# Stage changes without a meeting of engines, and the norm there in two halves of the tokens

## The chip, the cores and the metric

The kernel runs on one core of one Trainium2 chip. The metric is the device time of one execution in microseconds (us). The kernel before took 1945.89 us, the median of three runs (1944.5 to 1947.28).

## What is computed

Four layers of a small transformer, each with cross attention, self attention and a feed-forward part: twelve sublayers over 32 x 32 = 1024 tokens of width 256, all in fp32. Between sublayers the pattern is always the same:

```python
x = x + sublayer(_layernorm(x, axis=-1), ...)
```

The sublayers differ: softmax attention, an attention with query sets, capped attention, a "resonance" attention, and routed experts. Two details matter here. The first feed-forward part (`l0_feed_forward`) normalises the normed rows once more, by their root mean square, with a scale vector; it picks one of 8 experts by distance to centroids of those rows, and adds the result to the layer-normed rows and x. Some sublayers norm a second time with a mean and variance of their own, which for rows that are normed already is the same as another epsilon and factor in the first root.

## The kernel before, in words

The 1024 tokens stand as 8 tiles of 128 rows (`core.X`, [128, 8, 256]). Each sublayer is a *stage*: a Python function (`l0_cross`, `l0_self`, `l0_feed_forward`, then `l1_...`, `l2_...`, `l3_...`) that opens one block, in which each of the five engines has its own instruction stream. Semaphores order them. In this text the stages are called by their tile prefixes: l0x, l0a, l0f, l1x, l1a, l1f, l2x, l2a, l2f, l3x, l3a, l3f (x cross attention, a self attention, f feed-forward). There is no planner: the order on each engine is the order in which the code is written.

**The tail of a stage.** TensorE (PE) multiplies the last output projection, two tiles at a time. VectorE (DVE) adds each pair to X, and `Norm.take` (L227, L230) computes `bn_stats` and `bn_aggr` for these tiles, so that means and variances are ready when the stage ends. ScalarE (ACT) loads the table for the square root (`load_table`, L242). PE runs filler matmuls on constants (`keep_busy`, L83).

**The change of stage.** The end of a block is a meeting of all engines; `free_sems` (L89) then lets GpSimd (POOL) clear the stage's semaphores and makes all engines meet a second time.

**The head of a stage.** PE runs filler again. ACT takes the root of the variances of all eight tiles (`Norm.scalar`, L259), DVE the reciprocal (`Norm.deviations`, L237) and the shift (L195), and then both write the normed rows H: DVE five tiles (L197), ACT three (L206). PE transposes the rows tile by tile (`Flip.tensor`, L292) into four PSUM banks, ACT copies two of these to HT (L305, L309) and DVE the other two (L320, L324), and `Flip.ready` holds PE's first projection until all four copies are done. SyncE (SP) starts the loads of the next stage's weights behind the meeting.

**l0f.** Behind the H rows, ACT squares and sums them (L2089) and takes a root (L2091), DVE makes the rows R (L2111), PE transposes R, ACT squares R for its lengths (L2095), PE computes the distances (`route_tile`, L1253), and DVE and PE sort the tokens by expert (`Places`). DVE then adds H to X (L2131), POOL gathers the sorted rows with indirect DMAs (`move_rows`, L1023), and PE transposes them (L1054) ahead of the experts' matmuls.

**l2f.** Four pairs of experts in a hardware loop on PE and DVE; its tail does not call `take`, so the head of l3x computes the statistics of all eight tiles (L181, L217).

**l3x and l3a.** l3x multiplies a bias vector by the value weights (16 small matmuls, L3474) in front of the transposes. l3a norms twice: rows H for the values, then rows in `at.Q` for queries and keys, with a second transposition; its projections (L384 for queries and keys, L389 for values) run tile by tile in turn.

Of the kernel before, what the change touches and what calls it, by code (L numbers as in the profile page):

```python
# [26 lines left out]
ROWS_BY_DVE, ROWS_BY_ACT = (0, 2, 4, 6, 7), (1, 3, 5)  # L27
EXPERTS = {2: (8, 3072, 0), 5: (9, 5136, D), 11: (6, 2052, D)}
SHARED = 5
FIRST_PARTS = (0, 4 * D, 4 * D + 2 * D + 8 + P + 2 * B + 1 + C * B, 4 * D + 2 * D + 8 + P + 2 * B + 1 + C * B + 5 * D)  # L30


class Core:


    def __init__(self, nc, es, dram):
        self.nc, self.es, self.dram = nc, es, dram
        self.sems = []
# [4 lines left out]
        self.weights = [self.sb("weights0", [P, 6424]), self.sb("weights1", [P, 10640])]  # L43
# [6 lines left out]
        self.eps = self.sb("eps", [P, 3])  # L50
# [13 lines left out]
        self.eps5, self.eps10, self.eps6 = (self.eps[:, i:i + 1] for i in range(3))  # L64
        self.x_in = self.sem("x_in")
        self.shared_in = self.sem("shared_in")
        self.vectors_in, self.rest_in = self.sem("vectors_in"), self.sem("rest_in")
        self.norm = Norm(self)
        self.flip = Flip(self)
        self.ctx_norm = ContextNorm(self)  # L70
        self.sems = []
# [4 lines left out]
    def sem(self, name):  # L76
        self.sems.append(self.nc.alloc_semaphore(name=name))
        return self.sems[-1]
# [81 lines left out]
class Norm:  # L160
# [3 lines left out]
    def __init__(self, core):  # L164
        self.core = core
# [3 lines left out]
        self.uses_dve = self.uses_act = self.shifts_dve = self.shifts_act = 0  # L169
        self.taken = False  # L170

    def vector(self, dve, src, dst, rows_done):

        c, nc = self.core, self.core.nc
        if src is c.X and self.taken:
            dve.sem_inc(self.moments_done, 1)  # L176
            self.deviations(dve)
            self.taken = False
        else:
            for t in range(NT):  # L180
                done = nc.vector.bn_stats(c.stats[:, t, :], src[:, t, :])  # L181
            c.dve_step(dve, done)
            self.statistics(dve)
        self.rows(dve, src, dst, rows_done)

    def rows(self, dve, src, dst, rows_done):
        c, nc = self.core, self.core.nc
        if not isinstance(rows_done, tuple):
            for t in range(NT):
                nc.vector.tensor_scalar(dst[:, t, :], src[:, t, :], c.moments[:, t, 0:1], c.rstd[:, t:t + 1],  # L190
                                        ALU.subtract, ALU.mult).then_inc(rows_done, 1)
            return
        dve_done, _ = rows_done
        self.shifts_dve += 1
        nc.vector.scalar_tensor_tensor(c.shift[:], c.moments[:, :, 0], -1.0, c.rstd[:], ALU.mult, ALU.mult).then_inc(self.shift_done, 1)  # L195
        for t in ROWS_BY_DVE:
            nc.vector.tensor_scalar(dst[:, t, :], src[:, t, :], c.moments[:, t, 0:1], c.rstd[:, t:t + 1],  # L197
                                    ALU.subtract, ALU.mult).then_inc(dve_done, 1)

    def scalar_rows(self, act, src, dst, rows_done):  # L200
        c, nc = self.core, self.core.nc
        _, act_done = rows_done
        self.shifts_act += 1
        act.wait_ge(self.shift_done, self.shifts_act)
        for t in ROWS_BY_ACT:
            nc.scalar.activation(dst[:, t, :], src[:, t, :], ACT.Identity, bias=c.shift[:, t:t + 1], scale=c.rstd[:, t:t + 1]).then_inc(act_done, 1)  # L206

    def wait_rows(self, eng, rows_done):
        dve_done, act_done = rows_done
        eng.wait_ge(dve_done, len(ROWS_BY_DVE))  # L210
        eng.wait_ge(act_done, len(ROWS_BY_ACT))

    def statistics(self, dve):

        c, nc = self.core, self.core.nc
        for t in range(NT):
            done = nc.vector.bn_aggr(c.moments[:, t, :], c.stats[:, t, :])  # L217
        done.then_inc(self.moments_done, 1)
        self.deviations(dve)

    def take(self, dve, written, tiles):
# [7 lines left out]
        for t in tiles:  # L229
            nc.vector.bn_aggr(c.moments[:, t, :], c.stats[:, t, :])  # L230
        self.taken = True

    def deviations(self, dve):
        c, nc = self.core, self.core.nc
        self.uses_dve += 1
        dve.wait_ge(self.std_done, self.uses_dve)
        c.dve_step(dve, nc.vector.reciprocal(c.rstd[:], c.std[:]))  # L237
# [6 lines left out]
    def scalar_twice(self, act):  # L244


        self.scalar(act, self.core.eps10, 1 + 1e-5)

    def vector_again(self, dve, src, dst, rows_done):

        dve.sem_inc(self.moments_done, 1)
        self.deviations(dve)
        self.rows(dve, src, dst, rows_done)

    def scalar(self, act, eps, scale=1.0):
        c, nc = self.core, self.core.nc
        self.uses_act += 1
# [4 lines left out]
class Flip:  # L262
# [10 lines left out]
    def tensor(self, pe, src, rows_done, order=None):  # L273
# [3 lines left out]
        if self.uses["pe"]:  # L277
            self.ready(pe, "pe")
# [2238 lines left out]
def l1_self(core, load_next):  # L2517
# [20 lines left out]
    with ExitStack() as es:  # L2538
# [41 lines left out]
        def _(pe):  # L2580
# [79 lines left out]
            for m in range(FIRST):  # L2660
                project(m)
# [1428 lines left out]
```

## Time and profile before

| | |
|---|---|
| median of three runs | 1945.89 us |
| profiled execution, span from its first to its last instruction | 1943.1 us |
| TensorE, busy share of the span | 93% |
| DVE | 55% |
| ACT | 42% |
| POOL | 28% |
| mean granted TensorE clock | 0.971 |

The profile gives no time of its own for the profiled execution beyond the span; the span is 2.8 us below the median of the runs. The busy share of TensorE holds the filler matmuls and the time in which a matmul waits in its pipeline, so it isn't a share of useful work. A granted clock of 1.00 is 2.4 GHz and 0.50 is 1.2 GHz.

### The profile page before, as it was taken

The numbers are of one execution on the slowest core, as the hardware profiler recorded it, in microseconds if no ns is written. First come the engines' busy times: TensorE is split into PE (matmuls) and PEld (weight loads), VectorE is DVE, ScalarE is ACT, GpSimd is POOL, SyncE is SP. The second block draws the span as 40 slices with busy tenths as digits, with TensorE's granted clock in tenths as the row PEclk, the third lists the DMA queues.
The fourth block names the chain that finished last, engine by engine and source line by source line (L and its number), as shares of the span: only waits on it lengthen the run. The fifth ranks groups of instructions, "written<-read, shape, count | busy, mean of one in ns | idle before, by whom it ended". The sixth has DMA issues, their size and how long they took to land. (4 is left out here: it accounts for less than half of the span.)

```text
span 1943.1 us, 43256 instructions
## 1 busy us (share of the span) xinstructions
PE 1799.9 (93%) x16836; PEld 1400.7 (72%) x16836; DVE 1059.5 (55%) x2671; ACT 825.1 (42%) x2373; POOL 547.0 (28%) x586
## 2 busy tenths in 40 slices
PE   8999879999999989799999999999688899997898
PEld 6886568944777756699999967777454477755787
DVE  7786761163366437966555545555754555437511
ACT  6664521132166424333333335554510566626332
POOL 4440113200144302311222113332202456515242
PEclk9999778999999999999999999999799999998999
DMA  4110057662134110042899732111011345300397
GB/s 148 56 57 5 2 198 275 241 186 92 43 102 105 43 55 3 3 154 86 298 335 332 279 121 97 46 50 61 2 55 59 98 153 157 104 1 2 123 338 252
DMA packets 87010, 233.92 MB, mean 120 GB/s; under 512 B 9776, under 2 KB 45136, under 8 KB 80304
## 3 DMA queue, kind: packets, MB, share of 16 engines
q1 hardware_dynamic: 78992, 213.90, 32.5%
q0 software_dynamic: 5664, 15.47, 2.4%
q8 instruction: 121, 1.98, 0.4%
q10 hardware_dynamic: 2176, 2.10, 0.3%
q14 instruction: 57, 0.47, 0.1%
HBM read 216.21 MB, written 12.07 MB: 117 GB/s over the span
## 5 line engine op out<-in xcount | busy, mean ns | idle before, releaser
L2222 POOL TENSOR_TENSOR l1x_probs<-l1x_probs,l1x_total 128x512 f32<-128x512 f32 x64 | 65.1, 1038 | 203.7 <-DVE l1x_total L2461 203.7
L1541 PE MATMUL PS<-weights,l0x_ctxT 128*128 128x256 f32 x512 | 121.3, 387 | 0.0
L1074 PE MATMUL PS<-l1f_xT,l1f_slot 128*128 128x128 f32 x1024 | 117.0, 275 | 0.0
L1074 PEld LDWEIGHTS PS<-l1f_xT,l1f_slot 128*128 128x128 f32 x1024 | 115.7, 192 | 0.1
L83 PE MATMUL PS<-consts 128*128 128x256 f32 x366 | 90.8, 401 | 15.9 <-PEq L89 14.2
L1541 PEld LDWEIGHTS PS<-weights,l0x_ctxT 128*128 128x128 f32 x512 | 94.4, 191 | 15.2 <-issue 2.7
L2992 POOL TENSOR_TENSOR l2x_probs<-l2x_probs,l2x_total 128x512 f32<-128x512 f32 x64 | 65.0, 1038 | 127.1 <-DVE l2x_total L3182 127.1
L83 PEld LDWEIGHTS PS<-consts 128*128 128x128 f32 x366 | 72.3, 202 | 31.0 <-issue 18.3
L259 ACT ACTIVATE std<-moments,eps 128x8 f32<-128x8 f32 x13 | 3.9, 301 | 191.7 <-DVEq L176 122.3
L1201 DVE SCALAR_TENSOR_TENSOR l1f_product<-PS,l1f_slot,l1f_side 128x128 f32<-128x128 f32 x128 | 36.0, 344 | 65.9 <-ACT l1f_side L1157 65.9
L3496 PE MATMUL PS<-l3x_keysT,l3x_QW 128*128 128x289 f32 x256 | 67.7, 407 | 1.7 <-issue 1.7
L1028 POOL DMA_INDIRECT l1f_out_dram<-l1f_out,l1f_sort_target_row x23 | 22.7, 985 | 159.5 <-DVE l1f_out L1184 159.5
L1157 ACT ACTIVATE l1f_side<-PS,l1f_slot 128x128 f32<-128x128 f32 x128 | 36.5, 368 | 66.0 <-PE PS L1074 66.0
L1721 ACT ACTIVATE l0x_sq<-PS 128x256 f32<-128x256 f32 x128 | 47.8, 385 | 32.7 <-PE PS L1541 32.6
L3520 PE MATMUL PS<-tagged,l3x_QT 128*128 128x256 f32 x256 | 60.6, 380 | 0.9 <-ACT tagged L3610 0.9
L1074 PE MATMUL PS<-HT,weights 128*128 128x128 f32 x512 | 60.6, 280 | 0.9 <-DVE l1f_gated L1206 0.7
L3020 PE MATMUL PS<-l2x_ctxT,weights 128*128 128x257 f32 x256 | 61.1, 381 | 0.0
L1074 PEld LDWEIGHTS PS<-HT,weights 128*128 128x128 f32 x512 | 59.8, 196 | 1.7 <-DVE l1f_gated L1206 1.1
L1201 DVE SCALAR_TENSOR_TENSOR l1f_product<-PS,weights,l1f_side 128x128 f32<-128x128 f32 x120 | 33.8, 344 | 49.0 <-ACT l1f_side L1157 48.9
L3028 PE MATMUL PS<-weights,l2x_ctxT 128*128 128x256 f32 x256 | 60.4, 379 | 0.0
L3127 ACT ACTIVATE l2x_probs<-PS,l2x_top 128x257 f32<-128x257 f32 x128 | 59.2, 482 | 1.3 <-DVE l2x_top L3176 1.3
L1157 ACT ACTIVATE l1f_side<-PS,weights 128x128 f32<-128x128 f32 x120 | 34.2, 367 | 59.2 <-PE PS L1074 59.2
(663 smaller groups left out, 4630.9 us busy)
## 6 DMA issues: line engine op xcount, KB each, us to landing
l1f_slot<-in_experts_up_dram SPq DMA_DIRECT2D x16, 2056.0 KB, 10.5
weights<-in_experts_up_dram SPq DMA_DIRECT2D x8, 2056.0 KB, 10.4
weights<-in_experts_down_dram SPq DMA_DIRECT2D x21, 640.0 KB, 5.8
weights<-in_experts_up_dram SPq DMA_DIRECT2D x10, 1024.0 KB, 8.2
l1f_slot<-in_experts_down_dram SPq DMA_DIRECT2D x16, 640.0 KB, 4.8
l0x_ctxT<-in_ctxT_dram SPq DMA_DIRECT2D x32, 257.0 KB, 2.6
l1x_ctxT<-in_ctxT_dram SPq DMA_DIRECT2D x32, 257.0 KB, 2.9
l2x_ctxT<-in_ctxT_dram SPq DMA_DIRECT2D x32, 257.0 KB, 2.6
```

The costliest lines, as they stand in the source:

```text
L83: self.nc.tensor.matmul(self.PS[:, bank, 0:2 * P], self.ident, self.consts[:, 0:2 * P], start=True, stop=True)
L1074: done = nc.tensor.matmul(PS[:, bank + a, m * P:(m + 1) * P], mat[:, c, m * P:(m + 1) * P], x, start=(c == 0), stop=(c == 1))
L1157: nc.scalar.activation(self.side[u][:, m, :], PS[:, 2 * u, m * P:(m + 1) * P], ACT.Identity, bias=w["b1"][:, 4 * u + m:4 * u + m + 1]).the ...
L1201: done = nc.vector.scalar_tensor_tensor(p[:, m, :], PS[:, 2 * u + 1, m * P:(m + 1) * P], w["b3"][:, 4 * u + m:4 * u + m + 1], self.side[u] ...
L1541: last = nc.tensor.matmul(PS[:, 2 * (b % 2) + k, half * D:(half + 1) * D], ctxT[b % SLOTS][:, c, half * P:(half + 1) * P], kw[:, c, k * D: ...
L2222: nc.gpsimd.tensor_tensor(p, p, bcast(total[b % 2][:, 2 * n:2 * n + 2], 2, KEYS), ALU.mult).then_inc(probs_done, 1)
L2992: nc.gpsimd.tensor_tensor(p, p, bcast(total[b % 2][:, 2 * n:2 * n + 2], 2, 2 * P), ALU.mult).then_inc(probs_done, 1)
L3020: last = nc.tensor.matmul(PS[:, 4 + 2 * o, 0:CTX], wk[:, c, o * P:(o + 1) * P], ctxT[b % 2][:, c, :], start=(c == 0), stop=(c == 1))
L3028: last = nc.tensor.matmul(PS[:, 5, half * D:(half + 1) * D], ctxT[b % 2][:, c, half * P:(half + 1) * P], wv[:, c, :], start=(c == 0), stop ...
L3127: done = nc.scalar.activation(probs[b % 2][:, u, :], PS[:, u, 0:CTX], ACT.Exp, bias=top[b % 2][:, u:u + 1], scale=-1.0, accum_out=total[b ...
L3496: done = nc.tensor.matmul(PS[:, 2 * (b % 2) + u, 0:KEYS], QW[:, c, b, 4 * u:4 * u + 4, :].rearrange("p h q -> p (h q)"), keysT[b % 2][:, c ...
L3520: nc.tensor.matmul(PS[:, 6 + c, 0:2 * P], tokens[b % 2][:, half, c * P:(c + 1) * P], probsT[b % 2][:, half, :], start=(half == 0), stop=False)
```

## The change

It has five parts.

1. **No meeting.** All stages share one block. `leave` ends a stage: SP, ACT and DVE each drain and add one to a semaphore `left`, and POOL waits for the other four, clears the stage's semaphores, and adds one. PE adds its one behind the transposes of the first half (in `Flip.tensor`). `enter` waits for `left` before an engine first touches a semaphore of the new stage. Two ranges of semaphore numbers alternate. The last stage is not left.
2. **The norm by halves.** `Norm.take` signals after tiles 3 and 7. In the old stage's tail, DVE runs `early_vector` (reciprocal and shift for tiles 0 to 3) behind the third of its four additions, and ACT runs `early_scalar` (root, then the rows of tiles 0 to 3, all by ACT). In the new stage `scalar` and `vector` do tiles 4 to 7 (ACT tile 5; DVE tiles 4, 6, 7). PE transposes the first half at once; the projections of the first half come before the transposes of the second. Loops over (output, half) become loops over (half, output). In the three expert stages both halves are transposed before the router.
3. **Fillers.** `keep_busy` goes at the heads and tails of the stages, except 4 of 10 matmuls at the end of l0x; those inside the expert stages stay.
4. **l0f.** The second norm becomes part of the first root (another epsilon), the flip's copies multiply by the scale, POOL makes the rows R in two halves, and the addition of the layer-normed rows to X becomes eight `tensor_scalar` on POOL, in front of its gathers.
5. **Others.** l2f's last pair of experts is taken out of DVE's loop, with `take` in it. l3x's bias matmuls go behind the first context's work. l3a projects the values of tiles 0 to 3 ahead, and DVE alone writes the eight rows of the second norm. The start of the program is in the same block as l0x.

```diff
-ROWS_BY_DVE, ROWS_BY_ACT = (0, 2, 4, 6, 7), (1, 3, 5)
+ROWS_BY_DVE, ROWS_BY_ACT = (4, 6, 7), ((0, 1, 2, 3), (5,))
...
-    def free_sems(self):
-        self.nc.clear_and_free_semaphores(self.sems)
+    def enter(self, eng):
+        if self.stages:
+            eng.wait_ge(self.left, 5 * self.stages)
+
+    def leave(self):
+        nc, left, sems, others = self.nc, self.left, self.sems, 5 * self.stages + 4
+        @self.block.sync
+        def _(sp):
+            sp.drain().then_inc(left, 1)
...
+        @self.block.gpsimd
+        def _(pool):
+            pool.wait_ge(left, others)
+            nc.clear_and_free_semaphores(sems)
+            pool.drain().then_inc(left, 1)
         self.sems = []
-        self.nc.all_engine_barrier()
...
+    def early_scalar(self, act):
+        self.roots(act, self.use + 1, 0)
+        self.rows_by_scalar(act, self.use + 1, 0)
+
+    def early_vector(self, dve):
+        self.shifts(dve, self.use + 1, 0)
...
+    def project_tensor(self, pe, xT, wqk, wv):
+        flip = self.core.flip
+        flip.ready(pe, 0)
+        self.core.enter(pe)
+        self.project(pe, xT, xT, wqk, wv, (0, 1))
+        flip.tensor(pe, 1)
+        self.project(pe, xT, xT, wqk, wv, (2, 3))
+        flip.ready(pe, 1)
+        self.project(pe, xT, xT, wqk, wv, range(HALF, NT))
         self.turn_tensor(pe, 0)
         self.turn_tensor(pe, 1)
...
@@ l0_feed_forward, gpsimd
+            for half in range(2):
+                tiles = slice(HALF * half, HALF * half + HALF)
+                norm.wait_rows(pool, half)
+                nc.gpsimd.tensor_tensor(R[:, tiles, :], core.H[:, tiles, :], bcast(scale, 1, HALF), ALU.mult).then_inc(scaled, 1)
             ex.places.name_rows(pool)
+            pool.wait_ge(skips_done, 1)
+            for t in range(NT):
+                done = nc.gpsimd.tensor_scalar(core.X[:, t, :], core.X[:, t, :], more[:, t:t + 1], less[:, t:t + 1], ALU.mult, ALU.add)
+            done.then_inc(skipped, 1)
             ex.move_rows(pool)
...
@@ l1_cross, l3_cross and alike, tensor
-            pe.wait_ge(core.consts_in, 16)
-            core.keep_busy(7, 2)
+            flip.tensor(pe, 0)
+            core.enter(pe)
...
             for n in range(2 * HB):
-                o, half = n // 2, n % 2
+                half, o = divmod(n, HB)
+                if n == 2:
+                    flip.tensor(pe, 1)
+                if n == HB:
+                    flip.ready(pe, 1)
...
-            core.keep_busy(0, 4)
...
@@ l2_feed_forward, vector
+            add_pair(E // 2 - 1, 0)
+            dve.wait_ge(summed, (E // 2 + 1) * NT - HALF)
+            norm.take(dve, None, range(HALF))
+            add_pair(E // 2 - 1, 1)
+            norm.early_vector(dve)
+            dve.wait_ge(summed, (E // 2 + 1) * NT)
+            norm.take(dve, None, range(HALF, NT))
```

## Rows read from the trace of the kernel before

**Rows 1.** The page: span, busy time, and the group of the filler matmuls.
```profile
span 1943.1 us, 43256 instructions
PE 1799.9 (93%) x16836; PEld 1400.7 (72%) x16836; DVE 1059.5 (55%) x2671; ACT 825.1 (42%) x2373; POOL 547.0 (28%) x586
...
L83 PE MATMUL PS<-consts 128*128 128x256 f32 x366 | 90.8, 401 | 15.9 <-PEq L89 14.2
```

**Rows 2.** Windows, output to projection: us; PE, PEld, DVE, ACT, POOL busy; PEclk; DMA; GB/s.
```profile
177.00:189.00 12.00, 9.17 (x41) 7.16 (x39) 8.34 (x24) 4.29 (x12) 0.65 (x3) 0.86 0.04 14
253.00:265.00 12.00, 9.24 (x43) 6.85 (x42) 8.81 (x27) 5.13 (x21) 3.20 (x7) 0.95 0.77 308
382.00:401.00 19.00, 16.01 (x83) 13.59 (x81) 10.68 (x31) 3.44 (x6) 2.42 (x4) 1.00 0.40 124
693.40:700.60 7.20, 5.16 (x29) 3.64 (x28) 4.41 (x12) 2.99 (x6) 0.47 (x2) 1.00 0.45 148
826.60:832.70 6.10, 4.98 (x30) 3.68 (x28) 4.30 (x15) 2.85 (x6) 3.40 (x10) 1.00 0.41 121
1140.00:1148.20 8.20, 5.79 (x33) 4.03 (x32) 5.31 (x17) 3.42 (x7) 3.13 (x3) 1.00 0.22 68
1350.10:1357.40 7.30, 5.34 (x31) 4.02 (x29) 5.21 (x16) 2.99 (x6) 0.63 (x3) 1.00 0.50 160
1419.40:1427.00 7.60, 5.88 (x27) 4.64 (x26) 4.37 (x13) 3.08 (x7) 0.00 (x0) 0.82 0.54 203
1486.60:1500.30 13.70, 8.30 (x45) 7.19 (x45) 9.12 (x30) 3.49 (x7) 4.87 (x3) 0.88 0.56 176
1730.10:1741.70 11.60, 7.89 (x47) 5.78 (x46) 7.95 (x22) 6.34 (x12) 2.74 (x4) 1.00 0.01 2
1802.80:1810.00 7.20, 5.58 (x31) 4.03 (x29) 4.58 (x15) 2.86 (x6) 3.68 (x11) 1.00 0.10 36
```

**Rows 3.** Timeline, l1x to l1a: start, us, engine, line, operation.
```profile
694.40 0.18 DVE L230 BATCH_NORM_AGGREGATE moments<-stats 128x2 f32<-128x6 f32 x1
...
696.18 0.30 ACT L259 ACTIVATE std<-moments,eps 128x8 f32<-128x8 f32 x1 [21.62 <-DVEq L176]
...
696.95 1.59 ACT L206 ACTIVATE tagged<-X,shift,rstd 128x256 f32<-128x256 f32 x3 [0.47 <-DVE shift L195]
...
697.39 2.35 PE L292 MATMUL PS<-consts,tagged 128*128 128x128 f32 x16 [0.17 <-DVE tagged L197]
...
700.62 5.82 PE L2608 MATMUL PS<-HT,weights 128*128 128x512 f32 x13 [0.88 <-DVE HT L320]
```

**Rows 4.** Timeline, l2x to l2a: the third pair's moments.
```profile
1350.05 0.25 DVE L230 BATCH_NORM_AGGREGATE moments<-stats 128x2 f32<-128x6 f32 x2
```

**Rows 5.** Timeline, l0a to l0f: router, first gather, first transposition.
```profile
265.68 6.97 PE L1253 MATMUL PS<-l0f_centm,l0f_XT 128*128 128x8 f32 x32
...
286.48 3.14 POOL L1023 DMA_INDIRECT l0f_rows_in<-l0f_rows_dram,l0f_sort_token_row  x1 [27.43 <-DVE l0f_sort_token_row L858]
...
295.25 0.69 PE L1054 MATMUL PS<-consts,l0f_rows_in 128*128 128x128 f32 x2 [6.52 <-DMA l0f_rows_in<-l0f_rows_dram,l0f_sort_token_row]
```

**Rows 6.** L1023's gathers in l0f: from issue to landing.
```profile
DMA to landing us min/median/max: 2.8/6.8/8.7
```

**Rows 7.** Groups on POOL by form: busy, mean ns, idle before.
```profile
L1501 POOL TENSOR_SCALAR tagged<-X,moments,rstd 128x256 f32<-128x256 f32 x8 | 10.2, 1283 | 0.0
...
L3712 POOL TENSOR_TENSOR tagged<-tagged,weights 128x2048 f32<-128x2048 f32 x1 | 4.2, 4161 | 0.1
```

**Rows 8.** Timelines, l0f to l1x and l2f to l3x.
```profile
396.15 1.26 POOL L2216 TENSOR_SCALAR l1x_scaled_kv<-weights 128x128 f32<-128x128 f32 x2
...
1490.69 2.71 DVE L181 BATCH_NORM_STATS2 stats<-X 128x6 f32<-128x256 f32 x8 [2.22 <-PEq L89]
1491.63 1.84 PE L3474 MATMUL PS<-weights 128*128 128x1 f32 x16
```

**Rows 9.** Window inside l0a, columns as in rows 2.
```profile
216.00:233.00 17.00, 12.76 (x428) 9.51 (x428) 11.61 (x23) 13.58 (x29) 4.19 (x4) 0.50 0.01 3
```

More of the change, by code:

```diff
@@ L168, in __init__ @@
         self.shift_done = core.sem("norm_shift_done")
[L169 to L219, printed above, removed]
+        self.rows_act = core.sem("norm_rows_act")
+        self.rows_dve = core.sem("norm_rows_dve")
     def take(self, dve, written, tiles):
@@ L229, in take @@
         for t in tiles:
[L230 to L237, printed above, removed]
+            done = nc.vector.bn_aggr(c.moments[:, t, :], c.stats[:, t, :])
+        if tiles[-1] % HALF == HALF - 1:
+            done.then_inc(self.moments_done, 1)
     def load_table(self, act):
@@ new lines, in shifts, with rows_by_scalar @@
+    def shifts(self, dve, use, half):
+        c, nc = self.core, self.core.nc
+        tiles = slice(HALF * half, HALF * half + HALF)
+        dve.wait_ge(self.std_done, 2 * use + half + 1)
+        c.dve_step(dve, nc.vector.reciprocal(c.rstd[:, tiles], c.std[:, tiles]))
+        nc.vector.scalar_tensor_tensor(c.shift[:, tiles], c.moments[:, tiles, 0], -1.0, c.rstd[:, tiles], ALU.mult, ALU.mult).then_inc(self.shift_done, 1)
+    def rows_by_scalar(self, act, use, half):
+        c = self.core
+        act.wait_ge(self.shift_done, 2 * use + half + 1)
+        for t in ROWS_BY_ACT[half]:
+            c.nc.scalar.activation(c.H[:, t, :], c.X[:, t, :], ACT.Identity, bias=c.shift[:, t:t + 1], scale=c.rstd[:, t:t + 1]).then_inc(self.rows_act, 1)
@@ L327, in ready @@
-    def ready(self, eng, key, half=1):
-        eng.wait_ge(self.copied_act, 2 * self.uses[key] - 1 + half)
-        eng.wait_ge(self.copied_dve, 2 * self.uses[key] - 1 + half)
+        src, wait_row = c.H if src is None else src, wait_row or c.norm.wait_row
+        if nth:
+            self.ready(pe, half, nth - 1)
+        for ch in range(C):
+            for t in range(HALF * half, HALF * half + HALF):
+                if ch == 0:
+                    wait_row(pe, t)
+                last = nc.tensor.transpose(c.PS[:, 2 * half + ch, (t % HALF) * P:(t % HALF + 1) * P], src[:, t, ch * P:(ch + 1) * P], c.ident[:])
+            last.then_inc(self.flipped, 1)
@@ new lines, in tensor, with scalar @@
+        if half == 0 and nth == 0:
+            pe.drain().then_inc(c.left, 1)
+    def scalar(self, act, half, dst, scale=None, bias=None, nth=0):
+        c, nc = self.core, self.core.nc
+        act.wait_ge(self.flipped, 4 * (self.use + nth) + 2 * half + 1)
+        bank, to = c.PS[:, 2 * half, :], dst[:, 0, half * 512:(half + 1) * 512]
+        if scale is None:
+            last = nc.scalar.copy(to, bank)
+        elif bias is None:
+            last = nc.scalar.activation(to, bank, ACT.Copy, scale=scale[:, 0:1])
+        else:
+            last = nc.scalar.activation(to, bank, ACT.Identity, bias=bias[:, 0:1], scale=scale[:, 0:1])
+        last.then_inc(self.copied_act, 1)
@@ L2512, in _ @@
                 add_out(tiles)
+                if tiles == (4, 5):
+                    norm.early_vector(dve)
         cn.loads = B // cn.SLOTS
@@ L3526, in _ @@
             pe.wait_ge(q_copied, 2 * M)
+            for m in range(M):
+                for c in range(C):
+                    done = nc.tensor.matmul(PS[:, 7, m:m + 1], wv[:, c, m * P:(m + 1) * P], bm[:, c:c + 1], start=(c == 0), stop=(c == 1))
+            done.then_inc(v_bias_done, 1)
             for n in range(HEADS * C):
```

673 lines of the change are left out of this document (372 added, 301 removed).

## The prediction, as put on record before the result

> **What bounds the kernel now.** I read the page first. TensorE is busy for 93% of the span, no other engine for more than 55%, but 90.8 us of TensorE's time is filler on constants [rows 1]. So the question is where TensorE does nothing useful, and the change of stage is such a place, eleven times. The second view is the windows, each cut from a stage's last output matmul to the next stage's first projection [rows 2]. They hold 19.0 us at most (l0f to l1x, where most is the gather of the experts' rows), 6.1 at least (l1a to l1f) and 111.9 together. The only useful work of TensorE in one is 16 transposes (32 in l3a). The third view is the timeline of one change, l1x to l1a [rows 3]: the last moments are done at 694.58, the root starts at 696.18, because all engines meet twice in between, the transposes run from 697.39 to 699.74, and the first projection starts at 700.62, behind the last copy. The waits are in series, and TensorE is behind every one of them.
>
> **What limits TensorE behind the change.** From the last moments to the projection it is 6.0 us, and nothing of this can be hidden while the norm needs all eight tiles. With halves, the chain of tiles 0 to 3 can start when their moments are done, several us earlier. What then remains between the last output matmul and the first projection is: eight transposes (half of 1.9 to 2.4, so 1.0), one copy of 0.69 with its latencies, and beside the copy the leaving: DVE's and PE's drains, POOL's clearing, and the release of PE. The two meetings together take 1.6 us from the end of the moments to the start of the root [rows 3], and one of them goes, so I give the leaving 0.7 (bounds 0.5 and 1.6). The eight transposes of the second half now cost TensorE 1.0 behind the first projections, and that comes off each gain below, except where both halves stand ahead of the router.
>
> **Where TensorE ends late (l1a, l2f, l0a).** In l1a the rows of the first half are done before the last output matmul. The first projection is then at 693.4 + 1.0 + 1.1 = 695.5 in place of 700.6, less 1.0: a gain of 4.1. In l2f DVE's early reciprocal and shift fall in an idle stretch; the rows end at about 1420.8, the transposes at 1421.3, DVE's last moments at 1421.3, the projection starts at 1422.4 in place of 1427.0: 4.6 less 1.0, so 3.6. In l0a ACT's rows end near 182.1 and the projection starts at 183.8 in place of 189.1: 4.3.
>
> **Where DVE's last pairs run back to back (l2x, l2a, l1x).** Here the rows of the first half can only start behind the third pair, and the last pair is put back by 0.45 (reciprocal and shift). For l2a: third moments at 1350.3 [rows 4], shift done 1350.7, four rows by ACT at 0.53 each (three took 1.59 [rows 3]) to 1352.8, transposes to 1353.3, release 0.7, projection at 1354.1 in place of 1357.4: 3.3, and 2.5 are left, because DVE has one more copy between its rotations. l2x by the same steps: 1145.0 in place of 1148.2, less 1.0: 2.3 with rounding. l1x is the poor one. PE leaves only behind the transposes, at about 396.7, POOL clears then, and only then prepares the key weights, 1.46 us of memset and two multiplications (the latter 1.26 [rows 8]), which a matmul in front of the projections needs. That puts the projections at 399.5 in place of 401.0, less 1.0: 0.5. SP's loads of context also wait for POOL, about 1.4 us longer than before; I cost this at nothing because TensorE has 16 projections of some 0.86 us and the hidden layer in front of that context; if this cover is gone it is 1.4.
>
> **Where both halves come first (l1f, l3f).** Only the meetings and half of the rows are saved. The second half goes on from the end of DVE's last moments: root 0.35, reciprocal and shift 0.45, three rows 1.1, transposes 0.4, copies. The router can start on tiles 0 to 3 after the first copy: 1.8 in l1f, 2.2 in l3f.
>
> **l3x.** l2f's statistics (2.71 for eight tiles [rows 8], and the aggregates) leave the head. Rows by ACT from 1488.9 to 1491.1, transposes to 1491.5, first projection at 1492.5 in place of 1500.3: 7.8. Less 1.0 for the second transposes and less 1.84 for the bias matmuls, which lay in the shadow and are now on TensorE's path [rows 8]: 5.0. **l3a.** TensorE first does four value projections (1.03 each), but DVE alone makes eight rows at 0.34, and the queries and keys start at 1739.3 in place of 1741.6. DVE limits this phase, so the value work taken off TensorE isn't counted: 2.5.
>
> **l0f.** The squares, the second root and DVE's eight rows (3.26) leave the chain. POOL makes R instead: half of 4.16 each [rows 7], so 255.6 to 260.1, and ACT's squares of R end at 261.9. The router runs from 258.8 and takes 3.7 at full clock (as in l3f's head) or 7.0 at half as before, so it ends between 262.5 and 265.8; before, it ended at 272.65 [rows 5]: 6.9 to 10.2 gained. Part of this is given back: the eight `tensor_scalar` on POOL stand in front of its gathers. The nearest row is a POOL operation of this shape with two column operands, 1.28 us [rows 7], so 10.3 us, where DVE's one addition was 2.3 us and beside the path. The first gather was issued at 286.48 and its rows came at 295.2, 8.8 later, while the experts' weights were loading and DVE wrote [rows 5]. Now the issue stands 0.5 (three small DVE operations) and 10.3 us further behind the sorting, but the weights will have landed, and a gather lands 2.8 us from issue at the least [rows 6]: 0.5 + 10.3 + 2.8 - 8.8 = 4.8 lost. Net 3.5 (bounds 1 and 6). The Trainium skill, page GPSIMD Engine Reference, section 4.1 Engine selection, puts elementwise work on VectorE and calls GpSimd about two times slower for two inputs; by its measured 4.5 to 2.3 us for 2048 elements the eight would take 4.5 us, the gathers would hardly be late, and l0f would gain 8 to 9. The row of this shape says 10.3, and I go by the row.
>
> **Start and end.** One meeting at the start, and one meeting with a clearing at the end go: 1.0 (bounds 0.5 and 1.6).
>
> **The sum.** 4.3 (l0a) + 3.5 (l0f) + 0.5 (l1x) + 4.1 (l1a) + 1.8 (l1f) + 2.3 (l2x) + 2.5 (l2a) + 3.6 (l2f) + 5.0 (l3x) + 2.5 (l3a) + 2.2 (l3f) + 1.0 = 33.3 us.
>
> **The clock.** The fillers go, and with them activity of TensorE around each change. Even with them, the clock stood at half in four of eleven windows: 0.86 over 12.0 us is 3.4 us at 1.2 GHz [rows 2], and 16 transposes then took 3.7 in place of 2.35. So one such fall costs 1.4 to 1.7. The gaps that remain are shorter (2.5 us or less of idle), but nothing fills them. I count four more falls: 6 us. None is the lower bound, and in all eleven, with l0f longer, about 15 the upper. The Trainium skill, page TensorE: Matmul & The Clock Gate, section Why this matters for your kernels, says to keep TensorE free of gaps between bursts because an idle gap halves the clock; by that rule a fall follows each of the seven clean changes, 12 us in place of 6.
>
> Net 33.3 - 6 = 27.3. The profiled span would be 1943.1 - 27.3 = 1915.8. The median of the runs is 2.8 above the span, so 1918.6.
>
> **The rivals.**
> *The clock stays down (slower).* Without the fillers TensorE starts every stage cold and stays so in the attention phases, where its work is thin. That such a phase can stay at half for long is shown: 17 us at 0.50 in the middle of l0a [rows 9], with filler at its ends. Where TensorE limits, x us at half clock cost x/2. The point from which it decides is 33.3 / 11 = 3.0 us lost per change, 6 us more at half. At 12 us more at half it is 66 lost, so 1945.9 + 33 = 1979. Against it: seven windows at 1.00 with up to 1.9 us of unfilled idle. Chance 0.06.
> *More falls than I count.* All changes fall and l0f stays down longer: 15 lost, 1945.9 - 18 = 1928. Chance 0.16.
> *The head start is eaten.* Stages in which DVE, ACT or the context loads set the pace (l1x, l2a, l3a, l3x) end where they did: of the sum 0.5 + 2.5 + 2.5 + 5.0 fall away, 1929. For it: l3a's rotation runs at DVE's 3.4 us a tile. Against: DVE too starts earlier there. Chance 0.12.
> *The releases do nothing.* POOL's clearing waits for the slowest engine, so `left` could be a meeting under another name: then only the early rows gain, about 0.9 us less at each change, and with the clock 1928 again; if the first half's rows too come late, within 0.2% of before. Chance 0.04 for this last.
> *Better than the sum.* POOL is quick in l0f, and no clock falls: 1945.9 - 33 - 5 = 1908. Chance 0.10.
> The forecast, 1912 to 1925, keeps 0.52.
>
> **Numbers.** A difference under 0.2% (3.9 us) can't be told from none here. Faster: 0.52 + 0.16 + 0.12 + 0.10 = 0.90. Within 0.2%: 0.04. Slower: 0.06. The range leaves out the cold clock, the empty case and the ends of the others: 1906 to 1932.
>
> **What the profile of the changed kernel would show.** ACT's four rows ahead of the last moments; the windows shrunk to 2 to 4 us (l1a 7.2 to about 2.1 ahead of the first projection); transposes of the second half behind two projections without a wait on DVE; in l0f the router ending by 266, then POOL busy for 10 us ahead of the first gather, whose rows arrive near 293; granted clock of 0.5 for some 3 us at more changes than four. Wrong would make it: stretches of half clock of 10 us and more behind the changes, a wait of TensorE on POOL's clearing above 1.5 us, or TensorE waiting for the second half's copies.

## The result, and the profile after

The changed kernel took 1930.64 us (median of 4 runs, 1926.96 to 1933.89), the kernel before 1946.59 (4 runs, 1944.5 to 1951.67), timed beside it: ratio 0.9915, 95% interval 0.9897 to 0.9933, some 16 us faster. The forecast was 27.3 us and 1918.6. The time lies inside the range, at its upper end, and outside the 1912 to 1925 that I gave the likeliest case. It is nearest to the rivals "the head start is eaten" (1929) and "more falls than I count" (1928), which the time alone can't tell apart. The profiled execution was the slowest of the four, with a span 11.0 us below that of before.

The page of the changed kernel, span, busy time, the granted clock in 40 slices, and the group of fillers (answers to [rows 1]):

```profile
span 1932.1 us, 42749 instructions
PE 1783.8 (92%) x16692; PEld 1382.3 (72%) x16692; DVE 1056.5 (55%) x2665; ACT 836.0 (43%) x2389; POOL 551.8 (29%) x596
...
PEclk9999879999999999989999999999799999997899
...
L91 PE MATMUL PS<-consts 128*128 128x256 f32 x222 | 55.0, 408 | 0.0
```

144 fillers less are 35.8 us less of TensorE's busy time, but its whole busy time fell by 16.1 only. So useful work takes longer. I call *gap* what lies between the start of a stage's last output matmul and the start of the next stage's first projection (in l0f, l1f and l3f of the router; in l3a of the first projection of queries and keys, so that four value projections lie in that gap), and *time at half clock* what the trace's clock records show at 0.50 within the span. The windows of the changed kernel have the lengths of its gaps; all are cut 0.29 us ahead of these starts (columns as in [rows 2]):

```profile
176.00:183.45 7.45, 4.67 (x20) 3.06 (x18) 6.26 (x20) 4.32 (x13) 0.00 (x1) 0.87 0.00 0
249.88:259.06 9.18, 4.50 (x23) 2.73 (x21) 7.96 (x15) 6.04 (x19) 5.10 (x5) 0.87 0.59 220
375.64:393.16 17.52, 14.76 (x71) 12.21 (x70) 9.26 (x29) 3.94 (x8) 2.43 (x4) 1.00 0.26 80
689.15:691.75 2.60, 1.54 (x12) 1.17 (x10) 1.68 (x5) 0.88 (x2) 0.14 (x1) 1.00 0.00 0
819.51:824.34 4.83, 3.05 (x19) 2.41 (x18) 3.34 (x11) 1.69 (x4) 1.99 (x7) 0.89 0.26 55
1135.62:1141.29 5.67, 3.52 (x16) 1.55 (x14) 4.20 (x17) 3.46 (x7) 0.57 (x2) 0.95 0.03 3
1346.73:1351.44 4.71, 2.42 (x12) 1.19 (x10) 3.29 (x13) 2.85 (x6) 0.09 (x1) 1.00 0.00 0
1415.26:1419.18 3.92, 2.76 (x12) 1.58 (x10) 2.35 (x7) 2.62 (x6) 0.00 (x0) 0.74 0.00 0
1481.06:1488.71 7.65, 3.49 (x11) 1.48 (x9) 4.75 (x16) 3.04 (x6) 0.40 (x1) 0.79 0.00 0
1723.61:1733.01 9.40, 8.20 (x52) 6.81 (x50) 7.45 (x23) 5.96 (x14) 2.85 (x4) 1.00 0.01 1
1793.71:1799.24 5.53, 4.44 (x19) 3.01 (x18) 3.94 (x13) 3.82 (x9) 0.93 (x4) 0.71 0.01 4
```

Cut in the same way from start to start, the eleven were 116.6 us before and are 78.5: 38.1 us gone. But the eleven stages behind them are 27.6 us longer, and l0x 0.4 shorter. Of this, 8.6 us were in the forecast (six times 1.0 for second transposes, 0.8 in l2a, 1.84 for bias matmuls). The rest stands behind the windows. Windows over the first work of four stages:

```profile
183.45:192.00 8.55, 8.27 (x23) 4.89 (x24) 3.32 (x10) 2.61 (x6) 0.79 (x3) 0.71 0.08 20
824.34:838.00 13.66, 13.66 (x71) 13.66 (x70) 4.83 (x20) 1.91 (x4) 6.47 (x8) 0.54 0.51 167
1419.18:1424.00 4.82, 4.53 (x9) 2.39 (x10) 1.25 (x6) 0.60 (x1) 0.00 (x0) 0.50 0.88 315
1488.71:1495.00 6.29, 6.00 (x16) 3.09 (x17) 4.70 (x6) 1.86 (x4) 4.58 (x3) 0.72 0.89 226
```

TensorE is busy in nearly all of each, so here each us at the lower level costs about half a us of useful work. The plainest row is l1f's router, 32 matmuls (TensorE's timeline, changed kernel):

```profile
822.83 2.00 PE L306 MATMUL PS<-consts,tagged 128*128 128x128 f32 x8 [1.78 <-DVE tagged L267]
824.62 6.83 PE L1281 MATMUL PS<-weights,HT 128*128 128x8 f32 x32
```

Before, the same 32 took 3.71 us, behind a window at 1.00 [rows 2, fifth line]:

```profile
832.65 3.71 PE L1253 MATMUL PS<-weights,HT 128*128 128x8 f32 x32
```

By stage, gap and stage together, with the time at half clock:

| | gap + stage before, us | after | difference | forecast | more at half clock |
|---|---|---|---|---|---|
| l0x and start | 176.70 | 176.29 | -0.4 | -0.5 | 0 |
| l0a | 75.74 | 73.89 | -1.9 | -4.3 | 0 |
| l0f | 129.56 | 125.76 | -3.8 | -3.5 | -3.4 |
| l1x | 311.07 | 313.51 | +2.4 | -0.5 | +6.8 |
| l1a | 133.17 | 130.36 | -2.8 | -4.1 | +3.4 |
| l1f | 313.48 | 316.12 | +2.6 | -1.8 | +10.2 |
| l2x | 210.06 | 211.10 | +1.0 | -2.3 | +3.4 |
| l2a | 69.30 | 68.52 | -0.8 | -2.5 | +3.4 |
| l2f | 66.38 | 65.80 | -0.6 | -3.6 | +3.4 |
| l3x | 244.27 | 242.55 | -1.7 | -5.0 | +6.8 |
| l3a | 73.11 | 70.10 | -3.0 | -2.5 | +6.8 |
| l3f and end | 140.21 | 138.05 | -2.2 | -2.7 | +3.4 |

The forecast's column holds no clock. All together the time at half clock grew by 44 us, from 113 to 157. Stage by stage the two don't run together: l0a fell 2.4 us short with nothing new at half clock, and l3a did better than forecast with 6.8 us more, in a stretch some 20 us behind its gap where the kernel before was at half too.

### The profile page after: what moved, and what is told of

Read it like the earlier page. It is cut to its first block, busy times and chain, and to the rows that moved or that the text cites. A ratio compares the mean times of both kernels' runs of the same rounds, so it can differ in the third digit from the quotient of the medians.

```text
span 1932.1 us, 42749 instructions
## 1 busy us (share of the span) xinstructions
PE 1783.8 (92%) x16692; PEld 1382.3 (72%) x16692; DVE 1056.5 (55%) x2665; ACT 836.0 (43%) x2389; POOL 551.8 (29%) x596
## 4 chain that ended last, share of the span: by engine, by line
PE 78%; DVE 9%; issue 4%; DMA 3%; ACT 3%; POOL 2%; ACTq 0%; SPq 0%; PEldq 0%; POOLq 0%; DVEq 0%; PEld 0%
PE PS L1100 15%; PE PS L1569 6%; PE PS L1111 5%; PE PS L3579 3%; PE PS L3402 3%; PE PS L3084 3%; PE PS L3604 3%; PE PS L3092 3%; PE PS L2310 3%; PE PS L2659 2%; PE PS L2336 2%; PE PS L2363 2%; PE PS L2347 2%; PE PS L3117 2%; PE PS L2289 2%
## 5 line engine op out<-in xcount | busy, mean ns | idle before, releaser
L1100 PE MATMUL PS<-l1f_xT,l1f_slot 128*128 128x128 f32 x1024 | 117.0, 275 | 0.0
L2310 PE MATMUL PS<-HT,weights 128*128 128x512 f32 x128 | 57.3, 608 | 2.2 <-DVE l1x_AT L2475 2.2
L3402 PE MATMUL PS<-weights,HT 128*128 (+1 forms) x128 | 58.0, 610 | 1.4 <-DVE HT L330 1.0
L2435 ACT ACTIVATE l1x_probs<-PS,l1x_top 128x257 f32<-128x257 f32 x128 | 59.2, 483 | 0.0
```

The lines of the kernel that those rows point to most:

```text
L1100: done = nc.tensor.matmul(PS[:, bank + a, m * P:(m + 1) * P], mat[:, c, m * P:(m + 1) * P], x, start=(c == 0), stop=(c == 1))
L2310: done = nc.tensor.matmul(PS[:, 2 * (n % 2) + g, :], ff1[:, c, (g * HB + m) * P:(g * HB + m + 1) * P], core.HT[:, c, half * 512:(half + 1) ...
L3402: last = nc.tensor.matmul(PS[:, t, :], core.HT[:, c, t * P:(t + 1) * P], experts[:, c, columns], start=(c == 0), stop=(c == 1))
```

## The experiments

All were timed in three groups (runs 1 to 4, 5 to 7, 8 and 9), each on a chip of its own with its own runs of the kernel before (medians 1943.4, 1943.3 and 1944.9 us). A ratio is always to the kernel before of the same group, as it stands on record with its interval; it isn't the quotient of the two medians, which would be 0.9957 for run 1, 1.0088 for run 5 and 0.9888 for run 7. So differences of 0.1 to 0.2% between ratios are soft. Stages, gaps and time at half clock come from the one traced execution of each run.

**1. The changed kernel again**, unchanged.

> The changed kernel itself, unchanged, beside the others of this call. Both theories: ratio to the kernel before 0.9915, within 0.9897 to 0.9933; some 150 to 160 us of the span at half clock, against 113 before.

1935.06 us, ratio 0.9938 (0.9914 to 0.9962), a little above the range expected, as is its time at half clock of 167 us. The runs of one kernel spread by 11 us here, and the clock goes with it: from span and mean clock of each run (time at half = 2 x (1 - clock) x span), the 19 runs of the kernel before in this group have 97 to 129 us at half and 1938.6 to 1953.2 us, with a slope of 0.42 us per us (correlation 0.96). The other two groups' runs of the kernel before give 0.39 (17 runs, 0.87) and 0.27 (11 runs, 0.65).

**2. Fillers around the transposes at the head of every stage behind l0x**, and at the tails of l2x (5) and l2f (12).

```diff
         if nth:
             self.ready(pe, half, nth - 1)
+        if fill:
+            c.keep_busy(2 * half + 1, fill[0])
         for ch in range(C):
             for t in range(HALF * half, HALF * half + HALF):
                 if ch == 0:
                     wait_row(pe, t)
+                    if fill and t > HALF * half:
+                        c.keep_busy(2 * half + 1, 1)
```

> The changed kernel with filler matmuls put back where TensorE idles around the change of stage (ahead of and between the transposes of the first half, in the expert stages of the second half too, and at the end of l2x and l2f). Theory A (the missing gain is the clock, because the fillers are gone): time at half clock falls from about 157 us to below 130, and the kernel gains 5 to 10 us on the changed one, ratio to before 0.986 to 0.989. Theory B (the missing gain lies in the order of the second half: its transposes, copies and rows wait): the time at half clock may fall, but the kernel stays within 3 us of the changed one.

1933.22 us, ratio 0.9934 (0.9909 to 0.9959): not told apart from run 1. The time at half clock fell from 167 to 96 us (162 to 108 as means over all their runs), below that of the kernel before, and the stages became shorter (l1f 310.1 to 306.5, l0f 117.0 to 113.5), but the gaps grew from 77.5 to 89.3 together (l1f 4.54 to 8.39, l3f 5.58 to 8.28, l3x 7.65 to 9.02). TensorE takes its instructions in order, so a filler that starts as a row arrives holds the transpose up. Theory A was right on the clock, and the time is as theory B had it, though not by its reason: the clock was bought at its own price.

**3. The meeting back, the halves kept.**

```diff
         def _(pool):
             pool.wait_ge(left, others)
             nc.clear_and_free_semaphores(sems)
             pool.drain().then_inc(left, 1)
+        for queue in (self.block.sync, self.block.scalar, self.block.vector, self.block.tensor):
+            @queue
+            def _(eng):
+                eng.wait_ge(left, others + 1)
```

PE's own drain moves from the transposes into `leave`.

> The changed kernel with a meeting of all five engines at each change of stage (each drains and waits for GpSimd's clearing before its first instruction of the new stage), halves and early rows kept. Theory C (the release of TensorE, DVE and ACT past each other is worth what I priced, the copies of the first half beside the leaving): 0.9 us more at each of 11 changes, so 8 to 12 us slower than the changed kernel. Rival (the semaphore is a meeting under another name): within 3 us of the changed kernel.

1948.91 us, ratio 1.002 (1.0003 to 1.0038). Against run 1 that is 0.8%, 16 us. The gaps are 92.7 us together, 15.2 more. With every engine in a meeting, the early rows bring nothing that survives the loss of the fillers. The 16 us are more than the 8 to 12 expected; these runs also have 15 us more at half clock than those of run 1 (means 177 and 162), so some 4 to 6 of the 16 can be the clock, at 0.27 to 0.42 us per us.

**4. l0f's eight additions on DVE**, behind the sorting, in place of POOL.

```diff
-            pool.wait_ge(skips_done, 1)
-            for t in range(NT):
-                done = nc.gpsimd.tensor_scalar(core.X[:, t, :], core.X[:, t, :], more[:, t:t + 1], less[:, t:t + 1], ALU.mult, ALU.add)
...
+            dve.wait_ge(skips_done, 1)
+            for t in range(NT):
+                done = nc.vector.tensor_scalar(core.X[:, t, :], core.X[:, t, :], more[:, t:t + 1], less[:, t:t + 1], ALU.mult, ALU.add)
```

> The changed kernel with l0f's eight operations on X done by DVE instead of GpSimd, beside the gathers instead of in front of them. In the changed kernel's trace they take 4.3 us in front of the gathers, and the first gathered rows come 11.0 us behind the sorting, against 9.6 before. Theory A and B alike: the first gather is issued about 5 us earlier, but DVE writes beside it and the experts' weights are still loading, so the rows come 1 to 3 us earlier; ratio 0 to 0.0015 below the changed kernel's. If my forecast of l0f had been right in kind (4.8 us lost by these operations) it would be 4 us or more.

1932.04 us, ratio 0.992 (0.9894 to 0.9947), not told apart from run 1 as a whole. By its trace, l0f behind the gap is 115.4 us in place of 116.6 and 117.0 in the two traces of the changed kernel: 1.2 to 1.6 won. The timelines show why not more. The changed kernel:

```profile
279.08 0.17 DVE L888 CAST l0f_sort_token_row<-l0f_sort_found_row 128x15 uint32<-128x15 f32 x1
...
280.62 4.30 POOL L2106 TENSOR_SCALAR X<-X,l0f_more,l0f_less 128x256 f32<-128x256 f32 x8 [20.07 <-DVE l0f_more L2173]
285.10 1.20 POOL L1049 DMA_INDIRECT l0f_rows_in<-l0f_rows_dram,l0f_sort_token_row  x1 [0.17 <-issue]
...
290.23 0.69 PE L1080 MATMUL PS<-consts,l0f_rows_in 128*128 128x128 f32 x2 [7.85 <-DMA l0f_rows_in<-l0f_rows_dram,l0f_sort_token_row]
```

And this run:

```profile
281.10 0.17 DVE L888 CAST l0f_sort_token_row<-l0f_sort_found_row 128x15 uint32<-128x15 f32 x1
...
282.14 1.20 POOL L1049 DMA_INDIRECT l0f_rows_in<-l0f_rows_dram,l0f_sort_token_row  x1 [19.58 <-DVE l0f_sort_token_row L888]
...
287.89 0.44 PE L1080 MATMUL PS<-consts,l0f_rows_in 128*128 128x128 f32 x2 [3.49 <-DMA l0f_rows_in<-l0f_rows_dram,l0f_sort_token_row]
291.00 0.66 PE L1080 MATMUL PS<-consts,l0f_rows_in 128*128 128x128 f32 x2 [2.66 <-DMA l0f_rows_in<-l0f_rows_dram,l0f_sort_token_row]
```

From the end of the token list to the first rows it is 11.0 us with the eight operations ahead of the gathers and 6.6 without, but without them the second group of rows comes 3.1 us behind the first (1.15 in the changed kernel), and TensorE waits there.

**5. The kernel before without its fillers** at the heads and tails of the stages (18 calls like this one; at the end of l0x 4 of 10 matmuls stay).

```diff
         @block.tensor
         def _(pe):
             pe.wait_ge(core.consts_in, 16)
-            core.keep_busy(7, 2)
+            pass
```

> The kernel before, its meetings and whole-norm order kept, but without the filler matmuls at the heads and tails of the stages (only four of the ten at the end of the first stage stay). It tells what the fillers were worth where the changes of stage are long. Theory A (their loss is what the change paid for with): the time at half clock grows from 114.6 us by 50 or more, the gaps between output matmul and projection stay near 117 us together (fillers run in idle time) and the time is 8 to 20 us above the kernel before, ratio 1.004 to 1.010. Rival: the half clock falls where TensorE waits for others anyway; the time at half grows, but the time itself stays within 0.2%.

1960.32 us, ratio 1.0066 (1.0043 to 1.0089): 12.8 us slower. The gaps are 120.6 us together (116.6 with fillers), the time at half clock 188 us (113). So fillers were worth 8 to 17 us where the changes of stage were long, and the rest of the change, set against this kernel and not against the one before, is worth 1.0066 - 0.9938 = 1.3%, 25 us. Set against this kernel, run 3 (meeting kept) and run 6 (no head start on half the tokens) are each 0.46%, 9 us, faster.

**6. Both halves transposed ahead of the first projection**, in all stages, without the meeting.

```diff
             flip.tensor(pe, 0)
+            flip.tensor(pe, 1)
...
-                if n == 2:
-                    flip.tensor(pe, 1)
```

> The changed kernel, with no meeting, but in the eight stages where TensorE projects between the two halves it transposes the second half right behind the first, ahead of the first projection. So the second half's rows are waited for as in the kernel before. It tells what starting on half the tokens is worth by itself. By my forecast the second half's rows come 0.5 to 2.5 us behind the first's in l1a, l2f, l0a, l2a, l2x, l3x: 1.5 us per stage and eight stages, so 8 to 14 us slower than the changed kernel, about level with the kernel before or up to 0.2% faster; the gaps grow by 8 times 2 to 3 us (their transposes now lie in them) and the stages shrink by 1.0 each. Theory B (the second half costs as much behind the projections as it saves): within 4 us of the changed kernel, and the durations of the stages shrink by 1.5 or more each.

1949.14 us, ratio 1.002 (1.0006 to 1.0034): 0.8% above run 1, 16 us. The gaps are 95.8 us together, 18.3 more than in run 1. Windows, columns as above, for the changes to l1a and to l3x:

```profile
688.76:693.03 4.27, 2.51 (x18) 1.89 (x17) 2.95 (x9) 1.49 (x3) 0.47 (x2) 1.00 0.35 65
1487.87:1501.14 13.27, 5.59 (x19) 3.04 (x17) 9.45 (x21) 3.64 (x7) 4.98 (x3) 0.65 0.37 92
```

l1a loses 1.7 us of gap, l3x 5.6 (part of that by the slow rows of run 8). So projections on four tiles are the cover under which the other four are normed. "The second half costs as much as it saves" is refuted. The stages did not shrink by 1.0 each as expected (1679.1 us together, 1678.1 in run 1), at 17 us more at half clock.

**7. Fillers only where run 2 gained by stage** (l0a, l0f, l1x, l2f, and 4 ahead of the second half in l1f), and run 4's edit.

```diff
-            flip.tensor(pe, 0)
+            flip.tensor(pe, 0, fill=(6, 1))
```

This is l0a; l0f has (2, 1) and (5, 1) for its halves, l1x (0, 1), l2f (2, 1), l1f (4, 1) for its second. In l2f's tail TensorE also runs 12 fillers ahead of the last sums.

> The changed kernel with fillers only at the heads of l0a, l0f, l1x and l2f and ahead of the second half in l1f (4), where the run with fillers everywhere gained (by stage: 2.2, 4.2, 1.0, 1.0 and 0.5 us), none where it lost (l1a, l2x, l3x), and with the eight additions of l0f on VectorE (1.2 to 1.6 us in the run that had only this). If the stages add up, 8 to 10 us below the changed kernel, so ratio 0.989 to 0.990 to the kernel before, time at half clock 110 to 130 us. If the clock falls move elsewhere when one place is filled (theory: one fall per dip, wherever), the gain is under 4 us.

1921.5 us, ratio 0.9878 (0.9854 to 0.9902), 1.2% faster than the kernel before and, its interval clear of run 1's, 0.6% or 11.7 us faster than that run of the changed one. Against the changed kernel's first measurement (0.9915, 0.9897 to 0.9933) it is 0.4%, 7 us, and the intervals just touch; all three are from different groups. The time at half clock is 106 us in place of 167. Windows on l0a, l0f and, with the router in it, l1f:

```profile
176.84:184.68 7.84, 6.88 (x36) 5.74 (x35) 6.39 (x22) 4.04 (x12) 0.27 (x2) 1.00 0.01 2
247.27:255.60 8.33, 8.22 (x48) 6.89 (x47) 5.54 (x15) 3.75 (x9) 4.24 (x2) 1.00 0.46 161
818.95:832.00 13.05, 12.82 (x115) 12.68 (x114) 6.85 (x28) 5.88 (x13) 5.77 (x5) 1.00 0.51 173
```

Its timeline for l1f's router stands against 6.83 us above:

```profile
818.42 0.71 PE L310 MATMUL PS<-consts,tagged 128*128 128x128 f32 x5
818.97 3.64 PE L1285 MATMUL PS<-weights,HT 128*128 128x8 f32 x32
```

l1f's gap and stage are 311.8 us in place of 316.1 and 314.6 in the two traces of the changed kernel, at a gap 0.7 to 1.0 longer.

**8. Run 7 with POOL's clearing in l3x behind the norm's rows.**

```diff
+            norm.wait_rows(pool)
             nc.gpsimd.memset(rest[:], 0.0).then_inc(zeros_set, 1)
```

> The light-filler kernel with one edit: in l3x GpSimd's clearing of 128x4096 elements (3.51 us) waits until the norm's rows are written, and so no longer runs beside VectorE's three rows. If GpSimd's writes are what makes these three rows take 4.39 us in place of 1.05, they fall to 1.1 to 1.6 us, the second half's transposes start 0.8 us earlier or go back to back with the two projections, and l3x shrinks by 0.5 to 1.5 us; the time as a whole by under 2 us, not to be told from none. Rival (the rows wait for something else, such as ScalarE's row or the copy's port): the three rows stay above 4 us.

1923.64 us, ratio 0.9892 (0.9874 to 0.9911), not told apart from run 7; nor is l3x shorter in its trace (242.9 us against 242.1, with 3.4 us more at half clock). The local effect is plain. The changed kernel, l3x:

```profile
1488.31 3.51 POOL L3797 MEMSET l3x_rest<- 128x4096 f32 x1 [77.37 <-POOLq L118]
...
1489.05 4.39 DVE L267 TENSOR_SCALAR tagged<-X,moments,rstd 128x256 f32<-128x256 f32 x3
```

This run, DVE and POOL:

```profile
1476.45 1.05 DVE L267 TENSOR_SCALAR tagged<-X,moments,rstd 128x256 f32<-128x256 f32 x3
...
1477.62 3.51 POOL L3804 MEMSET l3x_rest<- 128x4096 f32 x1 [77.58 <-DVE tagged L267]
```

**9. The changed kernel with fillers only in l0a and l0f.**

> The changed kernel with fillers only around the transposes at the heads of l0a (6, and one between rows) and l0f (2 and 5, and one between rows); the rest as in the changed kernel. Adding by stage from the run with fillers everywhere: 2.2 + 4.2 = 6.4 us faster than the changed kernel, time at half clock less by 20 to 25 us. If what one filler saves comes back as a fall elsewhere, under 2 us.

1931.6 us, ratio 0.9927 (0.9903 to 0.9951), not told apart from run 1. By stage l0a is 71.7 us (73.9 and 73.7 in the changed kernel) and l0f 123.3 (125.8 and 126.2): 2.1 and 2.7 won, 4.8 of the 6.4 expected. The time at half clock is 147 us, 10 to 21 less. But the traced span is only 1.0 to 1.6 us shorter than the two of the changed kernel: the other stages are together 3.5 us longer (l2a 69.5 against 68.5 and 67.0). Whether the clock's falls came back there or this is the spread between traces isn't told apart, so this run doesn't decide between its two theories.

## Why the prediction was right in its sign and too large in its size

**The gaps: right, a little too large.** For the ten changes without l0f the steps of the prediction give 37.4 us less of gap (its gains with the 1.0 and 1.84 put back); measured are 34.1. No one is off by more than 0.6, but nine of the ten fall short, 3.3 us together. l1a is the clearest: first projection 2.6 us behind the last output matmul, 2.1 being the forecast. What sets it isn't POOL's clearing. The changed kernel's timeline, l1x to l1a (answers to [rows 3]):

```profile
689.76 0.93 PE L306 MATMUL PS<-consts,tagged 128*128 128x128 f32 x7
...
690.29 0.58 ACT L317 COPY HT<-PS 128x512 f32<-128x512 f32 x1 [3.21 <-PE PS L306]
690.31 0.43 DVE L213 BATCH_NORM_STATS2 stats<-X 128x6 f32<-128x256 f32 x1
690.78 0.18 DVE L216 BATCH_NORM_AGGREGATE moments<-stats 128x2 f32<-128x6 f32 x1
...
691.10 0.69 DVE L330 COPY HT<-PS 128x512 f32<-128x512 f32 x1
...
692.04 3.67 PE L2659 MATMUL PS<-HT,weights 128*128 128x512 f32 x8 [1.35 <-DVE HT L330]
...
695.55 1.04 PE L306 MATMUL PS<-consts,tagged 128*128 128x128 f32 x8
```

DVE's copy stands behind DVE's last moments, so the projection starts 0.25 us after the copy; the release that I put at 0.7 is under it. The second half's 1.04 us of transposes lie behind two projections, as forecast.

**The release against the early rows.** I gave the meetings about 0.9 us a change, some 10 in all, and the early rows the rest. Runs 3 and 6 take away one each, and each loses 0.8%, 16 us. They aren't terms that add: above the kernel without fillers each alone is worth 9 us at most and both together 25 (runs 3, 5, 6 and 1). My reading, not shown by a trace: an early row is of use only if its engine isn't held at a meeting, and a freed engine only if it has work that doesn't wait for the second half.

**The clock: the term that was too small.** The forecast's step was "one such fall costs 1.4 to 1.7 ... I count four more falls: 6 us". The time at half clock grew in nine of the eleven stages, not in four; and I had sized a fall by a window, where TensorE idles half of the time, while most of the time at half now lies behind the windows, on projections and the router, where TensorE is the bound. In the profiled pair 38.1 - 8.6 + 0.4 = 29.9 us should have been won and 11.0 were, so 18.9 are left for the clock and for all else that I didn't foresee. In the medians, 16 won, it is 14.

How much of this is the clock is bounded, not measured. The time at half grew by 44 us (profiled pair) or 51 (mean of the 8 runs of run 1, clock 0.958 against 0.9715). Three measures of its price:

- 0.27 to 0.42 us per us over the three groups of runs of the kernel before: 12 to 21 us. These runs differ by themselves, so the slope needn't be the clock's doing alone.
- Run 5, fillers out of the kernel before and nothing else: 12.8 us for 75 us more at half, 0.17 us per us: 7 to 9 us.
- Run 7 against run 1: 11.7 us, less the 1.2 to 1.6 of the edit on DVE, for 49 to 61 us less at half, 0.17 to 0.21 with the fillers' own delay in it: 7 to 11. Against the changed kernel's first measurement (7 us in place of 11.7, for 42 to 51 us less at half) it is 5 to 7.

All but the last are above the forecast's 6. The two that rest on an edit give 5 to 11 of the 14, so the clock is the largest term that was too small, and with the 3.3 us of the gaps it closes the sum; that it is 14 by itself isn't shown. The forecast's own tell-tale, half clock of 3 us at more changes than four, came true. Of its three signs of being wrong, one came true in part and one in full: l1f has a new stretch of 13.7 us at half clock behind its gap (l0f's 17.1 was there before), and in l2x TensorE waits 1.5 us for a copy of the second half (below). The wait on POOL's clearing itself is 0.64 us at most (l2x).

Run 5 shows the same direction with nothing else changed. The Trainium skill, page TensorE: Matmul & The Clock Gate, section Why this matters for your kernels, says to leave TensorE no idle gap between bursts; the trace agrees in direction, with 44 us more at half clock. The page ties its rule to the length of the gap, and I had applied it to all seven clean changes alike, so that its 12 us come nearer than my 6 is luck in part.

**l0f: right in sum, two terms wrong that cancelled.** The net was forecast at 3.5 and is 3.8. But POOL's eight operations took 4.30 us, 0.54 each, not 10.3: the row that I went by [rows 7, first line] was of another stage. It was of the same shape and with two column operands too, but another pair of operations: subtract and multiply in l0x, multiply and add in l0f. DVE at work beside it isn't the reason, for one of the eight in l0x ran with DVE idle for all but its last 0.1 us and took 1.21 us all the same (kernel before, L1501 from 19.39, window on it, columns as in [rows 2]):

```profile
19.39:20.51 1.12, 1.12 (x51) 0.96 (x51) 0.00 (x0) 1.06 (x6) 1.12 (x2) 1.00 0.33 123
```

That the pair of operations makes the difference is not tested. The loss at the gathers is 1.4 us (token list to rows 11.0 us, 9.6 before), not 4.8. The router took 6.97 us at half clock again and ended at 266.3, 0.5 behind the late end of "262.5 to 265.8", and TensorE waited for DVE's rows (below). The 4.5 us that the prediction also gave stand in the Trainium skill, page GPSIMD Engine Reference, section 3.1 Elementwise — side-by-side cycle accounting, as measured for one addition of two tensors of 2048 elements; for eight operations with one tensor each it was an estimate. Measured are 4.30: nearer than the row, but for another kind of operation.

**l3x: 5.0 forecast, 1.7 seen**, with 6.8 us more at half clock, some 3.3 of it lost where TensorE is the bound, and DVE's three rows at 4.39 us in place of 1.05. **l1x and l2x** are dearer than forecast by 2.9 and 3.3 us, of which the clock explains up to 3.4 and 1.7. The loads of context, which I had put at nothing in l1x, cost nothing: TensorE waits for none of them there. The rest of l2x is a wait that I had put at nothing, of TensorE for the copy of the second half (changed kernel):

```profile
1141.70 4.50 POOL L3049 TENSOR_TENSOR X<-X,weights 128x2048 f32<-128x2048 f32 x1 [0.76 <-DVE tagged L267]
1142.23 4.25 DVE L3223 TENSOR_TENSOR l2x_last_rows<-l2x_last_raw,weights 32x256 f32<-32x256 f32 x1 [0.70 <-ACT l2x_last_raw L3173]
...
1148.08 0.68 DVE L330 COPY HT<-PS 128x512 f32<-128x512 f32 x1
1148.90 1.52 PE L3071 MATMUL PS<-HT,weights 128*128 128x512 f32 x3 [1.51 <-DVE HT L330]
```

DVE's operation on the last rows now stands ahead of its copy, and it ends only when POOL's multiplication does; before, it came behind all copies. The wait is 1.5 us in runs 1, 4, 7 and 9, 2.1 in run 3 and 2.9 in runs 2 and 8. So a part of the head start is eaten in l2x, a stage that the rival of that name didn't list. Of those that it listed, l3a kept its gain; in l1x, l2a and l3x the clock can cover what is missing, but no run shows that it does.

## What to carry to other kernels

Before a filler is removed, price it where its clock is spent: not in the gap that it fills but in the busy stretch behind that gap, and remove it alone once to see. Place fillers only where the engine would wait longer than they take; one that is in the queue when the data comes costs what it saves. Taking a meeting away and splitting the norm pay far more together than apart: each alone, without fillers, was no faster than the kernel before and 9 us faster than that kernel without fillers, both together 25 us. When work is moved behind a projection, look at what each engine has queued ahead of it there.

## What the runs showed that I had not expected

Some of VectorE's operations wait until GpSimd's operation beside them has ended. The clearest is the 32x256 `tensor_tensor` in l2x shown above: in all eleven traces it ends 0.27 or 0.28 us after GpSimd's multiplication of 128x2048, whenever it started, and so takes anything from 1.14 us (run 6) to 4.68 (runs 2 and 8). In l3x the three `tensor_scalar` on 128x256 took 4.39 us beside GpSimd's clearing of 128x4096 elements (the changed kernel): singly 2.91, 0.82 and 0.81, the first ending 0.14 us after the clearing, the other two beside two shorter operations of GpSimd. With the clearing moved (run 8) they took 1.05 together; the clearing took 3.51 either way. In l0f three took 2.91, the second of them 2.27, beside GpSimd's 128x1024 multiplication, and TensorE waited 1.54 us for them (changed kernel):

```profile
253.01 2.91 DVE L267 TENSOR_SCALAR tagged<-X,moments,rstd 128x256 f32<-128x256 f32 x3
...
253.20 2.25 POOL L2102 TENSOR_TENSOR l0f_R<-tagged,weights 128x1024 f32<-128x1024 f32 x1 [9.73 <-POOLq L118]
...
255.66 1.09 PE L306 MATMUL PS<-consts,tagged 128*128 128x128 f32 x6 [1.54 <-DVE tagged L267]
```

It isn't so for every operation: in the kernel before, eight `bn_stats` ran beside the clearing of 128x4096 at 0.34 us each [rows 8]. Only l3x was tested by moving the operation.

One kernel's runs differ by 11 to 15 us here, and mean clock and time go together (0.42, 0.39 and 0.27 us per us at half clock over 19, 17 and 11 runs of the kernel before, correlations 0.96, 0.87 and 0.65). For a change of 0.8%, the clock of each run belongs beside its time.
